# The four exponentials of a state in two pairs on ScalarE, with the first input pass of the slot between them

## What is computed

```
xc, z = split(norm(x) @ in_proj)            u = conv4(xc) + b
dt = clip(sigmoid(u @ dt_w + dt_b), 1e-4, 1)    B, C = u @ B_w, u @ C_w
per token:  dA = exp(clip(dt * A, -5, 5));  state = dA * state + dt*B*u + 1e-6
            y = sum_n(state * C) + D * u
x1 = x + (y * silu(z)) @ out_w
```

## Time and profile before

| | us |
|---|---|
| median of 3 runs | 3001.63 (2998.19 to 3005.22) |
| profiled execution | 2997.44 |
| its span | 2995.7 |
| busy: PE / PEld | 2625.7 (88%) / 2306.4 (77%) |
| busy: DVE | 2262.1 (76%) |
| busy: POOL | 2237.3 (75%) |
| busy: ACT | 2032.7 (68%) |

### The profile page before, as it was taken

How to read it: one execution, slowest core, us unless ns; L and a number is a source line. 1 busy time by engine, 2 the same in 40 slices (tenths; PEclk the granted TensorE clock), 3 DMA queues, 4 the chain that set the end, 5 groups by cost and what they waited for, 6 DMA issues and landing times. The chain is left out here.

```text
span 2995.7 us, 55801 instructions
## 1 busy us (share of the span) xinstructions
PE 2625.7 (88%) x15616; PEld 2306.4 (77%) x15616; DVE 2262.1 (76%) x4890; ACT 2032.7 (68%) x4675; POOL 2237.3 (75%) x1354
## 2 busy tenths in 40 slices
PE   7888888888888888888888888888886599999998
PEld 4777777777777777777777777777875488888887
DVE  2999899889998998999889989999899233333332
ACT  3978888878877777878887888888876023333332
POOL 2989898989898888888898989898887033333333
PEclk9898998899998988999999999999897699999999
DMA  4222222222222222222222222222221278888886
GB/s 172 78 75 75 76 82 76 75 76 86 94 77 76 79 75 84 85 75 83 79 79 75 75 77 82 75 76 83 94 72 43 75 195 200 199 201 200 199 201 154
DMA packets 138194, 309.69 MB, mean 103 GB/s; under 512 B 15040, under 2 KB 79680, under 8 KB 137792
## 3 DMA queue, kind: packets, MB, share of 16 engines
q1 hardware_dynamic: 110848, 270.03, 28.7%
q0 software_dynamic: 27072, 36.46, 6.1%
HBM read 258.42 MB, written 48.01 MB: 102 GB/s over the span
## 5 line engine op out<-in xcount | busy, mean ns | idle before, releaser
L1035 POOL TENSOR_TENSOR room<-dtu,b_all 128x1024 f32<-128x1024 f32 x512 | 1202.1, 2371 | 33.8 <-DVE dtu L1421 14.0
L814 ACT ACTIVATE bank<-room,eps_col 128x512 f32<-128x512 f32 x1024 | 693.7, 683 | 336.8 <-DVE carry L1258 229.9
L801 ACT ACTIVATE room<-room,neg_a 128x256 f32<-128x256 f32 x2048 | 868.4, 498 | 7.5 <-DVE room L1244 5.1
L607 PE MATMUL bank<-ident,room 128*128 128x128 f32 x4096 | 552.0, 291 | 246.9 <-DVE room L1253 219.9
L607 PEld LDWEIGHTS bank<-ident,room 128*128 128x128 f32 x4096 | 496.2, 151 | 300.8 <-DVE room L1253 238.3
L1024 POOL TENSOR_TENSOR room<-room,c_all 128x1024 f32<-128x1024 f32 x224 | 532.0, 2375 | 167.9 <-ACT carry L819 105.6
L1244 DVE TENSOR_TENSOR_SCAN bank<-room,carry,bank 128x256 f32<-128x256 f32 x864 | 580.8, 736 | 56.8 <-ACT bank L814 47.8
L1160 POOL DMA_INDIRECT out<-room,ids x144 | 223.8, 1554 | 406.5 <-ACT room L995 235.9
L1323 DVE SCALAR_TENSOR_TENSOR hid<-hid,bank 128x256 f32<-128x256 f32 (+1 forms) x312 | 131.0, 420 | 446.9 <-ACT hid L908 446.9
L1244 DVE TENSOR_TENSOR_SCAN room<-room,carry,bank 128x256 f32<-128x256 f32 x672 | 448.1, 726 | 12.0 <-ACT bank L814 10.7
L559 PE MATMUL bank<-xnT,w_conv 128*128 128x256 f32 x3072 | 404.2, 288 | 7.0 <-ACT xnT L837 5.5
(11 more groups left out here) (150 smaller groups left out, 3141.0 us busy)
## 6 DMA issues: line engine op xcount, KB each, us to landing
b_all<-b_scratch SPq DMA_DIRECT2D x128, 512.0 KB, 3.9
c_all<-b_scratch SPq DMA_DIRECT2D x128, 512.0 KB, 5.4
room<-in_wgu SPq DMA_DIRECT2D x72, 704.0 KB, 5.6
room<-in_wd SPq DMA_DIRECT2D x72, 384.0 KB, 3.5
room<-x_by_expert SPq DMA_DIRECT2D x72, 260.0 KB, 2.9
x_in<-in_x SPq DMA_DIRECT2D x32, 256.0 KB, 5.5
x<-in_x SPq DMA_DIRECT2D x32, 256.0 KB, 2.7
out<-x SPq DMA_DIRECT2D x32, 256.0 KB, 4.1
```

The lines of the kernel that those rows point to most:

```text
L607: last = mm(tr_bank[k][:, b * P:(b + 1) * P], v[n % VRING][:, b, k * P:(k + 1) * P], ident[:, :], is_transpose=True, start=False, stop=(n ...
L801: last = af(da[n % RING][:, b, :], dt[c.par][:, b, :], ACT.Exp, scale=neg_a[:, b, n:n + 1])
L814: af(v_slot(n, h)[:, :], v[n % VRING][:, 2 * h:2 * h + 2, :].rearrange("p b t -> p (b t)"), ACT.Identity, bias=eps_col[:, 0:1]).then_inc(v ...
L1035: nc.gpsimd.tensor_tensor(out=v[n % VRING][:, :, :], in0=dtu[:, :, :], in1=row, op=ALU.mult) \
```

## The change

On ScalarE, the four exponentials of state slot+3 are issued in two pairs (channel blocks 0 and 1, then 2 and 3), and the input pass of half 1 of state slot+1 stands between them instead of behind them. The wait for room in the ring stays at the first pair, the signal `da_ready` at the last exponential. The start-up, which makes the first decays of chunk 0, calls `decays` with all four blocks as before. No instruction is added or removed; the other engines' programs are the same.

```diff
--- before.py
+++ after.py
@@ -793,13 +793,15 @@
         def _(act):
             af = nc.scalar.activation
 
-            def decays(c, n):
+            def decays(c, n, blocks=(0, 1, 2, 3)):
                 if n == 0:
                     act.wait_ge(dt_ready, c.index * NT + NT)
-                wait(act, half_ready, halves(c, n - RING + 1))
-                for b in range(KD):
+                if 0 in blocks:
+                    wait(act, half_ready, halves(c, n - RING + 1))
+                for b in blocks:
                     last = af(da[n % RING][:, b, :], dt[c.par][:, b, :], ACT.Exp, scale=neg_a[:, b, n:n + 1])
-                last.then_inc(da_ready, 1)
+                if KD - 1 in blocks:
+                    last.then_inc(da_ready, 1)
 
             def add_eps(c, n, h):
                 act.wait_ge(v_mul, c.index * NS + n + 1)
@@ -943,12 +945,14 @@
                         return (None, 0) if not scan else (scan, n) if n < NS else (proj, n - NS)
 
                     for slot in range(NS):
-                        c, n = ahead(slot + DECAY_LEAD)
-                        if c:
-                            decays(c, n)
+                        far, m = ahead(slot + DECAY_LEAD)
+                        if far:
+                            decays(far, m, (0, 1))
                         c, n = ahead(slot + 1)
                         if c:
                             add_eps(c, n, 1)
+                        if far:
+                            decays(far, m, (2, 3))
                         if post:
                             finish(post, slot)
                         if proj:
```

## The result

| | before | after |
|---|---|---|
| median | 2999.91 us (4 runs) | 3096.34 us (4 runs, 3095.8 to 3096.56) |
| ratio | | 1.0321, 95% interval 1.0307 to 1.0335 |
| span of the profiled execution | 2995.7 us | 3094.8 us |

A forecast was written before the change was run, and what follows sets the result against it. VectorE, taking turns waiting with ScalarE, was taken to bound the kernel. Slots 11 to 14 add 94.3 us to the 2997.44 us profiled execution, giving 3091.7, rounded down to 3090 us; range 3035 to 3112 us.

The forecast's parts named there:

- VectorE is on the path: In the exponentials' stretch VectorE is busiest, 91%; time it loses lengthens the chunk unless it already stands idle there.
- The gains at states 7 and 9: VectorE's waits of 0.81 and 0.80 us at half 1 go, but TensorE's later outputs cover them: costed at 0.
- Slots 13 and 14: Pass waits for VectorE; the shared expert's tanh behind it comes later, adding 0.80 us each to VectorE's 0.40 us wait.
- Slot 12: Shared expert's tanh starts 1.52 us later behind the pair; 0.80 us stems from slot 11, so 0.72 us is new.
- Slot 11: The tanh of z follows the waiting pass; with the pair ahead it ends later and VectorE waits 0.80 us.
- Slot 5: The pair before the second norm lies in its 0.65 us wait for GpSimd: 0; at the high end 25 us.
- The 0.41 us of state 0: VectorE's gain at half 1 of state 0, expected to be waited off at state 7, so not subtracted.
- The sum: Slots 11 to 14 cost 3.12 us per chunk; 30 x 2.40 + 31 x 0.72 = 94.3 us in all.
- a follower of a waiting pass pays for the pair: Where ScalarE waits at the pass, the second pair delays the instructions behind it by 0.80 us, unless they have cover.

## Why the prediction was right

- **VectorE is on the path and its loss is idle time.** Right: busy times unchanged, 3.2 us more idle per chunk against 3.12 forecast.
- **The gains at states 7 and 9 are worth nothing.** Right: 1.35 us in slot 8 as forecast at 1.3, 0.75 us behind L639; pairs in slots 6 and 8 alone give 0.9996; with TensorE shortened they give 16 us. TensorE is not the only cover: with the pairs in slots 6 and 8 alone, 0.34 us of the gain of state 7 goes to ScalarE's next pass.
- **Slots 13 and 14, 0.80 us each.** Right: 1.19 us each, the pairs there alone cost 53 us against 48.
- **Slot 12, 0.72 us.** Right in size: 0.69 us per chunk where it was measured with slot 11.
- **Slot 11, 0.80 us.** Right in mechanism, too large: 0.56 us on average, as TensorE already held the tanh back in 9 of 25 chunks. I had rounded the sum down by 2 us for it; it is nearer 7 us.
- **Slot 5, taken as 0.** Wrong in size: alone it costs 19 us. The row that I read had a wait of 0.65 us for GpSimd, but of 25 chunks 8 had none, and the others 0.41 to 1.26 us. Weighed over all of them, a pair of 0.80 us sticks out by 0.37 us per chunk, 11 us; the rest of the 19 us is open.
- **The 0.41 us of state 0, not counted.** Not settled: 8 us less in the one comparison that isolates it, near the edge of what the runs tell apart.
- **The sum.** 94.3 us forecast, 96.4 us measured. That the sum is nearer than its terms is luck: slot 11 was some 7 us too large and slot 5 up to 19 us too small, both more than the difference of 2 us, and the parts measured alone overlap by 17 us. The step that carried the forecast, a follower of a waiting pass pays for the pair, is no luck: its waits stand in the trace at slots 11 to 14, in the size forecast or a little below.

## What to carry to other kernels

Moving an instruction to an earlier place in an engine's stream can pay only where it does not wait at the new place. Where it waits, it starts no sooner, and everything that it now precedes is late by the full length of what it passed; so name the follower of each wait before naming the gain. Read the cover of such a follower over all chunks, not in one: it was 0.65 us in the chunk read here and nothing in 8 of 25. A wait that two engines show for each other is no sign that it can be gained: look for the third engine that arrives at the same time a few slots on, and test with that engine's work cut.

## What the runs showed that I had not expected

Half of the dt projection's matmuls, 3.5 us of TensorE's time per chunk, are worth 51 us of 2999, 1.65 us per chunk, though TensorE stands idle at other times of the chunk (3.6 us ahead of the transposes in slot 0). And exchanging two neighbouring steps on ScalarE in slot 5 was worth some 29 us. Both point to where TensorE's chain starts and ends, which its share of busy time (88%) does not show.
